# One block for messages, cross attention and the last self-attention: one queue per engine, eight pooled PSUM banks, key roots as logarithm and exponential

## What is computed

```python
x = x + L0_xattn(layernorm(x), ctx, ...)     # 4 layers: self attention, cross attention, gated FFN
x = x + L0_attn(layernorm(x), U, V)          # messages
x = x + L0_ffn(layernorm(x), W, disha)       # x @ W.T + pooled @ disha
x = x + L1_xattn(ctx, layernorm(x), mask)    # 64 latents on 1601 context rows and themselves
x = x + L1_attn(layernorm(x), Wqkv, Wo)      # causal self attention, 16 heads
x = x + L1_ffn(layernorm(x), gate, w1, w2)   # 8 experts, top 2

# messages, C = 16 blocks of R = 64
u, v = (z @ U.T) * s, (z @ V.T) * s
qh = sigmoid(u_c @ v_c.T)
G = ((qh @ v) @ U + (qh.T @ u) @ V) * s
# L1 cross attention, per batch
xn = layernorm(ctx) * gx + bx                # 1601 x 128
k = rmsnorm(xn @ Wk) ; q = rmsnorm(ln @ Wq)
attn = softmax(where(mask, q @ k.T, -inf))   # 2 heads of 64
```

## Time and profile before

| | us |
|---|---|
| median of three runs | 670.51 (663.33 to 674.94) |
| the profiled execution | 668.31 |
| its span, from first to last instruction | 666.4 |
| layers (with set-up) | 0 to 258 |
| messages and FFN | 261 to 347 |
| cross attention | 347 to 555 |
| last self-attention | 555 to 594.5 |
| experts | 594.5 to 666.4 |

### The profile page before, as it was taken

The page is one execution under the profiler, slowest core; times in us unless marked ns, Lnnn a source line. Parts: engine busy times, 40 slices in busy tenths (PEclk is TensorE's granted clock), DMA queues, the critical chain, the costliest instruction groups (busy, mean ns, idle before and its releaser), DMA issues. The chain is left out here.

```text
span 666.4 us, 13787 instructions
## 1 busy us (share of the span) xinstructions
PE 566.7 (85%) x5334; PEld 437.1 (66%) x5334; DVE 373.7 (56%) x957; ACT 233.6 (35%) x544; POOL 262.7 (39%) x350
## 2 busy tenths in 40 slices
PE   0889998999999893988757999899898966959997
PEld 0666865866696673777645777677686754536676
DVE  4576676665457764365643677655645653634342
ACT  1366356445443651332213433222222321421210
POOL 3562372255125511035543576937537412400000
PEclk9999999997599997899985999575767976978999
DMA  5501011010620002101110001011000000000000
GB/s 154 222 1 30 17 50 29 18 48 1 190 94 2 1 2 60 73 2 53 52 50 1 1 1 50 0 50 49 3 1 1 1 0 2 1 1 1 0 2 17
DMA packets 8488, 22.20 MB, mean 33 GB/s; under 512 B 1248, under 2 KB 4152, under 8 KB 8160
## 3 DMA queue, kind: packets, MB, share of 16 engines
q1 hardware_dynamic: 8416, 21.23, 9.7%
HBM read 20.97 MB, written 0.26 MB: 32 GB/s over the span
## 5 line engine op out<-in xcount | busy, mean ns | idle before, releaser
L823 POOL TENSOR_TENSOR rstd<-ss,par 128x1 f32<-128x1 f32 x52 | 28.5, 549 | 107.8 <-ACT sq L675 107.6
L1212 PE MATMUL sc<-rope,pr 128*128 128x128 f32 x208 | 58.3, 367 | 0.0
L1426 POOL TENSOR_TENSOR rk<-rk,par 128x8 f32<-128x8 f32 (+1 forms) x32 | 45.7, 1427 | 2.7
L1212 PEld LDWEIGHTS sc<-rope,pr 128*128 128x128 f32 x208 | 35.9, 217 | 8.2
L1349 DVE TENSOR_TENSOR sd<-sc,rk 128x512 f32<-128x512 f32 (+1 forms) x32 | 18.9, 591 | 37.8 <-PE sc L1212 16.4
L1284 ACT ACTIVATE pr<-pt 128x512 f32<-128x512 f32 (+1 forms) x32 | 16.5, 515 | 61.8 <-PE pt L1201 61.7
L1201 PE MATMUL pt<-xw,pr 128*128 128x128 f32 x208 | 36.9, 328 | 0.0
L1227 PE MATMUL pt<-xh,sd 128*128 128x130 f32 x208 | 34.3, 327 | 1.5 <-ACT sd L1288 1.5
L1201 PEld LDWEIGHTS pt<-xw,pr 128*128 128x128 f32 x208 | 33.1, 237 | 2.2 <-issue 1.1
L692 ACT ACTIVATE pr<-sd 128x1024 f32<-128x1024 f32 (+1 forms) x36 | 31.2, 866 | 9.5 <-DVE sd L770 7.2
L1227 PEld LDWEIGHTS pt<-xh,sd 128*128 128x128 f32 x208 | 32.5, 241 | 2.6 <-issue 2.5
(11 more groups left out here) (255 smaller groups left out, 1394.3 us busy)
## 6 DMA issues: line engine op xcount, KB each, us to landing
cx<-ctx_in SPq DMA_DIRECT2D x8, 768.0 KB
we<-we_in SPq DMA_DIRECT2D x8, 514.0 KB, 8.4
wc<-wc_in SPq DMA_DIRECT2D x4, 768.5 KB, 5.6
wa<-wa_in SPq DMA_DIRECT2D x5, 387.0 KB, 3.0
wb<-wb_in SPq DMA_DIRECT2D x4, 256.5 KB, 3.6
uvT<-uvT_in SPq DMA_DIRECT2D x1, 1024.0 KB, 4.7
uv<-uv_in SPq DMA_DIRECT2D x1, 1024.0 KB, 6.9
xw<-xw_in SPq DMA_DIRECT2D x1, 323.0 KB
```

The costliest lines, as they stand in the source:

```text
L823: nc.gpsimd.tensor_tensor(rstd[:, t:t + 1], ss[:, t:t + 1], par[:, 1:2], ALU.pow).then_inc(s[piece], 1)
L1212: last = nc.tensor.matmul(part, xnT[n % 3][:, P * j:P * j + P], qp[:, i, :, :].rearrange("p h q -> p (h q)"), start=False, stop=True, skip ...
L1426: nc.gpsimd.tensor_tensor(rk[:, n, 0:2 * w], rk[:, n, 0:2 * w], par[:, 1:2].to_broadcast([P, 2 * w]), ALU.pow).then_inc(xm[piece], 1)
```

## The change

- The middle block and the last self-attention become one block with one sorted queue per engine. The table YAT now holds the messages, the FFN, the cross attention and the last self-attention: pieces of a tile that come before cross attention (HEAD) with a step of 20.883 per tile, pieces of a batch (XWAY) with 16.435 per batch, pieces of a tile behind it (TAIL) with 32.87 per tile, and the moments and the scaling of context rows with steps of their own. Layernorms are done tile by tile (z_, f_, x_, l_, n_ moments, power, norm).
- All eight PSUM banks are one pool: each user takes one bank, or two next to each other for the messages, project and turn, and waits for the last users of just these.
- The first layernorm of tiles 0 to 2 (z_*) moves into the queues of the layers; that of tile 3 is in the new block.
- The root of the keys: POOL keeps the floor (c_floor), ACT takes the logarithm and then exp(-x/2) (c_root), with one table load behind the last tanh.
- `top` becomes c_top: six tensor_tensor maxima, the first as soon as two groups are there.
- notm and sel have 128 partitions instead of 8, the rows past 8 being zero.
- c_normed of batches 3 to 7 is no longer tied to c_moments of the same load: these batches are loaded twice, once for the moments and once for the scaling (LOADS; 13 loads instead of 8).
- Buffers move: xnT into wa[1] and new tiles, sT into the space of uvT and uv, others into rope, kblk, sd and pr. All loads of the block wait until POOL has cleared 79 semaphores (64 before, when only the context rows waited).

The diff, cut to its core:

```diff
-XSTEP = 10.99
-XAT = {
+YSTEP = {"HEAD": 20.883, "XWAY": 16.435, "TAIL": 32.870, "MOMENTS": 20.974, "NORMED": 14.636}
...
+    "PE": {"z_turn": -75.33, "across0": -58.75, "along0": -47.11, "along1": -54.15, "across1": -55.67, "M0": -38.77,
...
         self.bank = {}
+        free, last = [float("-inf")] * 8, [()] * 8
+        for _, i, g, p in self.queue["PE"]:
+            n = next((n for n in YBANKS if p in YBANKS[n]), 0)
+            if n and (p, g) not in [("sum_ctx", k) for k in range(1, 4)]:
+                k = min(range(0, 8, n), key=lambda k: max(free[k:k + n]))
...
-        mraw = xsb("mraw", [B, CT * P], U8)
-        notm = xsb("notm", [B, CT * P], BF16)
-        sel = xsb("sel", [B, B, P], BF16)
+        mraw = xsb("mraw", [P, CT * P], U8)
+        notm = xsb("notm", [P, CT * P], BF16)
+        sel = xsb("sel", [P, B, P], BF16)
...
         def x_sp(sp):
+            sp.wait_ge(s["x_raised"], 1)
...
-            for b in range(B):
-                if b >= 2:
-                    sp.wait_ge(s["c_center"], 4 * (b - 2) + 4)
+            for u, (_, b) in enumerate(LOADS):
+                if u >= 2:
+                    kind, k = LOADS[u - 2]
+                    sp.wait_ge(xm["c_moments" if kind == "stats" else "c_center"], 4 * k + 4)
...
+            elif piece == "c_root":
+                x_wait(act, "c_floor", n + 1)
+                part = rk[:, n, 0:2 * width(g)]
+                nc.scalar.activation(part, part, ACT.Ln).then_inc(xm["c_log"], 1)
+                x_wait(act, "c_log", n + 1)
+                nc.scalar.activation(part, part, ACT.Exp, scale=-0.5).then_inc(xm[piece], 1)
...
-            elif piece == "c_rnorm":
+            elif piece == "c_floor":
                 x_wait(pool, "c_sums", n + 1)
...
-                nc.gpsimd.tensor_tensor(rk[:, n, 0:2 * w], rk[:, n, 0:2 * w], par[:, 1:2].to_broadcast([P, 2 * w]), ALU.pow).then_inc(xm[piece], 1)
...
-                nc.vector.tensor_reduce(mxp[i % 2][:], sT[i % 2][:, 0:CT, :].rearrange("p c q -> p q c"), AX, ALU.max).then_inc(xm["top0"], 1)
+                    last = nc.vector.tensor_tensor(mxr[:], tiles[0], tiles[1], ALU.max)
```

More of the change, by code:

```diff
@@ L108, in __init__ @@
     def __init__(self, engines, when):
-        self.queue = {e: sorted((when(p, l, t), l, t, p) for p, layers in pieces for l in layers for t in range(T))
+        self.queue = {e: sorted((when(p, l, t), l, t, p) for p, layers in pieces for l in layers for t in range(T)
+                                if p[:2] != "z_" or t < T - 1)
                       for e, pieces in engines.items()}
@@ L181 @@
 class CrossOrder:
     def __init__(self):
[L185 to L186 removed]
+        self.queue = {e: sorted((x_late(p, i, g), i, g, p) for p in pieces for i in x_range(p) for g in range(len(YENDS[p])))
+                      for e, pieces in YAT.items()}
         self.bank = {}
[L188 to L194 removed]
@@ L197 @@
-XORDER = CrossOrder()
+        free, last = [float("-inf")] * 8, [()] * 8
[3 more added lines that the diff above has]
+                k = min(range(0, 8, n), key=lambda k: max(free[k:k + n]))
+                ends = [(f, i, x_final(f, g)) for f in YBANKS[n][p]]
+                self.bank[p, i, g] = k, n, sorted({e for b in range(k, k + n) for e in last[b]})
+                free[k:k + n] = [max(x_late(*e) for e in ends)] * n
+                last[k:k + n] = [tuple(ends)] * n
@@ L216, in program @@
         pt = ctx.enter_context(nc.psum_tensor("pt", [P, 1024], F32))
-        small = [ctx.enter_context(nc.psum_tensor(f"small{i}", [P, 512], F32)) for i in range(2)]
+        sm = ctx.enter_context(nc.psum_tensor("sm", [P, 1024], F32))
+        small = [sm[:, 512 * i:512 * i + 512] for i in range(2)]
         x = sb("x", [P, T, D])
@@ L1113, in c_tiles @@
             return slice(CG[g][0], CG[g][-1] + 1)
+        LOADS = [("both", b) for b in range(XAHEAD)] + [("stats", b) for b in range(XAHEAD, B)] + [("norm", b) for b in range(XAHEAD, B)]
         def x_sp(sp):
+            sp.wait_ge(s["x_raised"], 1)
             sp.dma_start(xw[:], xw_in).then_inc(xw_loaded, 16)
@@ L1467, in x_pool_start, with x_queue @@
+        def x_queue(eng, piece_of, layer_of, engine):
+            fresh = False
+            for _, i, g, p in LAST.queue[engine]:
+                if p not in EARLY and not fresh:
+                    eng.wait_ge(s["x_raised"], 1)
+                    eng.sem_inc(s["x_seen"], 1)
+                    fresh = True
+                if p in SELF:
+                    layer_of(eng, LAST, p, LAYERS, i)
+                else:
+                    piece_of(eng, p, i, g)
         def x_pool_start(pool):
-            for i in range(2):
-                nc.gpsimd.memset(cx[i][:, CT - 1, :], 0.0).then_inc(s["c_zeroed"], 1)
@@ L1470, in x_pool_start @@
             raise_xm(pool)
             pool.sem_inc(s["x_raised"], 1)
+            for i in range(2):
+                nc.gpsimd.memset(cx[i][:, CT - 1, :], 0.0).then_inc(xm["c_zeroed"], 1)
             for i in range(3):
@@ L1646, in am_pool @@
-        def am_pool(pool):
-            layernorm_pool(pool, 1)
-            x_pool_start(pool)
-            layernorm_pool(pool, 2)
+            for i in range(T):
+                last = nc.gpsimd.memset(rope[:, i, 2:4, :], NEG)
+            last.then_inc(xm["sl_set"], 1)
         with nc.Block() as block:
```

806 lines of the change are left out of this document (391 added, 415 removed), and 3 rows, old and new, of the table YBANKS.

## The result

The changed kernel takes 585.84 us, median of 4 runs (574.18 to 592.98), beside 668.82 us of the kernel before, median of 4 (663.33 to 674.94). Every ratio in this document is of the fast executions alone (here 0.864, 95% interval 0.851 to 0.878), not of the medians (0.876), which are of all executions and in a later set include two odd ones, 1614.23 us of the kernel before and 1574.75 us of the changed one. The profiled execution of the changed kernel took 592.78 us, its span is 590.7. The last G and the first mask matmul start 0.1 us apart; B is counted from the mask matmul, C from the last scores to the experts' layernorm.

A forecast was written before the change was run, and what follows sets the result against it. It took TensorE's idling and half clock (109 us), blamed on GpSimd's powers, as what could be won. First products at 277 + 68 + 136 + 40 + 71.9 = 593, with 1.9 around the span 595; forecast 596 us, range 565 to 636.

The forecast's parts named there:

- B: Stretch from the last tile's G to the last scores: 119 us of TensorE work, 136 us in time, range 122 to 152.
- C: Stretch from the last scores to the experts' layernorm: 40 us, range 36 to 48, against 58.5 before.
- The mask: Mask matmuls on 128 partitions: mask and score pair 0.33 us instead of 0.58, saving 25.5 us of TensorE.
- rival that the type is the cost: Mask matmuls keep their price because bf16 stands between fp32: 29 us more, 625 us; chance 0.11.
- The start: New block's start to first message products: context load issued at 266.5, first products at about 277 us, range 274 to 281.
- A: Stretch from first message products to the last tile's G: 59 us of TensorE at density 0.87, 68 us; range 62 to 74.
- denser than I think: Rival: TensorE 0.95 dense from first message products to last scores, 62 + 125 us; 579 to 565 in all; chance 0.06.
- Experts: The experts, from their layernorm to the end, stay as they are: 71.9 us.
- GpSimd: GpSimd's work from 258 us on falls from 159 to 113 us, as it loses 45.7 us of powers.
- What bounds the kernel before: Cross attention before: GpSimd, slowed by 45.7 us of powers, falls behind, TensorE stands, and the clock goes to 1.2 GHz.
- c_top: Maximum over context tiles as six pairwise maxima: about 2.7 us per batch against 3.3, saving 5 us on VectorE.
- The rival of the falling clock: TensorE idles at pooled banks or VectorE's queue, clock falls to 1.2 GHz: 40 us more, 636 us; chance 0.11.

The follow-up runs named there:

- both small edits undone: The changed kernel with the mask and its selector on 8 partitions and the key root as a power on GpSimd again: 602.3 us, ratio 0.910.

## Why the prediction was right, and where it was not

The whole, 596 (565 to 636), was near the measured 585.84, in part by luck, as the sum below shows. The sign, the worth of the mask and the full clock in B were right; what the prediction named as the cause of the idling before was not. By its steps:

- **The mask** (0.33 us per pair, 25.5 us of work, bounds 0 and 31): right. 0.33 measured, B 23.6 us longer without it. The rival that the type is the cost is out: the pair of bf16 and fp32 on 128 rows takes 0.33 us, the 0.107 of a transpose and the 0.225 of an fp32 product, and nothing between. The rule of the Trainium skill (TensorEngine Tiling (Array Packing), Key Properties) on draining at a change of mode agrees: 0.25 us is what the change of rows costs here per pair, there and back. That the cost is such a drain no run shows.
- **The start** (first products about 16 us behind the block's start): 19.1 measured. The step that failed is the price of the clears: 3.6 us assumed for 79, 5.1 measured (280.08 to 285.18); and mask and selector, which the change makes sixteen times larger, go ahead of the context in the DMA queues (2.1 us, by the run with 8 rows), so the load took 6.5 us from its issue (287.37 to 293.90) and not 4.5. "TensorE need not wait for the layernorm" holds for tiles 0 to 2; tile 3's power held VectorE 7.08 us ahead of the load, and once the load came early that wait set the start. The 277 us were missed by 22, of which 4 are this (25.3 us from the layers' last matmul instead of 21.2) and 18 the layers.
- **A** (68 us from the first products to the last G): 63.9. TensorE was busy 62.87 of 64.00 in it, not 0.87.
- **B** (119 us of work, 136 in time): 115.9 of work, 118.4 in time. This is the mis-sized term, by 18 us: I took the density between that of the layers and of the messages, 0.87, and it was 0.98. The case "denser than I think" was the nearer one for B (125) and A (62), and put too low at 0.06.
- **C** (40 us): 36.9. **Experts** 71.9: 72.3.
- With the measured 291.5 us behind the first products (63.9 + 118.4 + 36.9 + 72.3) the start I forecast gives 277 + 291.5 + 1.9 = 570. The layers of the profiled execution took 18 us more and the start 4, and the median of the four lies between: two errors of opposite sign, the layers' scatter and B, put 596 so near, and that is luck.
- **GpSimd** (113 us of work): 118.4. **ScalarE** (64 activations at 0.25): 0.20 to 0.21 each, 13.1 us in all. The table load, taken at 1 us, is in ScalarE's timeline of the changed kernel:

```profile
350.23 1.28 ACT L1390 ACT_TABLE_LOAD   x1
```

  The Trainium skill (ScalarE: Activation LUTs, What ACT_TABLE_LOAD costs) makes up its 2.7 us of about 1.28 us of load and 1.38 us of drain. The load agrees; the drain can't be seen here, since ScalarE then waits 2.77 us for TensorE (until 354.28), so that the switch held nothing up.
- **What bounds the kernel before** is where the argument was wrong. I read three waits of 8.0 us and 33.89 of 50 busy us as "GpSimd is the slow one", which "falls behind", so that "TensorE stands, and the clock goes to 1.2 GHz". Both steps fail. With GpSimd's powers gone from the old kernel nothing moved. And in the trace of before the order is the other way: the clock fell at 414.4, after 50.47 busy of 51.40 us, and the first wait came behind it. TensorE, then GpSimd, in the kernel before:

```profile
409.66 1.06 PE L1201 MATMUL pt<-xw,pr 128*128 128x128 f32 x8
...
415.16 2.07 PE L1201 MATMUL pt<-xw,pr 128*128 128x128 f32 x8
...
420.07 1.09 PE L1195 MATMUL small<-cf,xh 128*128 128x128 f32 x4 [2.63 <-POOL xh L1160]
```
```profile
415.04 0.20 POOL L1145 TENSOR_TENSOR rsx<-mvx,par 128x13 f32<-128x13 f32 x1 [4.12 <-DVE mvx L1139]
```

  The same eight instructions for the keys take twice as long before TensorE has waited as much as 1 us for anything. Of the four falls between 413 and 513 us three (414.4, 445.1, 503.2) came ahead of such a wait and one (475.8) inside it. GpSimd itself stood idle ahead of all three waits, 4.12, 8.72 and 11.84 us, for VectorE's moments of the context, which stood in VectorE's queue behind the 3.00 us maximum; no run tests that order by itself. The busy column had said what was the bound: 90.69 of 100 us of TensorE in the very stretch at 0.64, beside 61.02 of GpSimd. GpSimd became one only when the merged order and the mask had brought TensorE to 15 us per batch, which is why the root is worth 0.2 us alone and some 21 at the end. For the changed kernel "GpSimd's 11 us per batch against TensorE's 15" had the right order and too high a figure: 68.26 and 115.91 us over eight batches are 8.5 and 14.5.
- **c_top** (2.7 us, 5 us of VectorE saved): 3.65 us per batch measured, more than the 3.3 of the old form; its gain is the 3.6 us at the very end.
- **The rival of the falling clock** (636): did not come. B ran at 1.00. The Trainium skill (TensorE: Matmul & The Clock Gate, A second HAM failure mode: psum-queue depth-cycling) would have the pooled banks make the clock swing; this trace does not show it. The longest wait of TensorE in B was 0.5 us.
- **The merging** itself is the largest part: 402.4 to 334.3 us with both small edits undone, 68 of the 92 us; 18 of them lie ahead of the first mask matmul, 29 from there to the last scores, 22 in C, and the experts took 1 more. In the windows above TensorE's work at full clock, busy time by granted clock, is 128 us from first mask to last scores before, and 139 in the merged block with both edits undone, where the other tiles' self-attention runs beside the batches; and it took 173 and 144 us. The mean clock went from 0.79 to 0.98, and C, with one tile instead of four, went from 58.5 to 36.8. What in the merging does this stays open: one queue, pooled banks, layernorms tile by tile, the earlier moments and the second loads came together and none was taken out alone. That the density keeps the clock up was argued from both kernels' traces, not tested; the fall at 414.4 in dense work speaks against it as the whole reason.

## What to carry to other kernels

Count busy time and granted clock together before an engine is named the bound: one that is 91% busy at 0.64 is it, and a few short waits for another engine are not evidence against that. Look at what the awaited engine was itself waiting for, and whether the clock fell before the wait or after it. Where two engines need nearly the same time per step, an edit's worth must be tried with and without the other: here each alone brought 2 to 3 us and the pair 24. Here a wait at the head of a queue shrank when the chain behind it started sooner; moving the waiting work down the queue only moved the wait.

## What was not expected of the hardware

**Half clock in dense stretches.** The layers' own code differs in time by up to 25 us from execution to execution (in the ten traces with the merged block its first transpose comes between 255.5 and 280.1 us), and the granted clock tells where. The changed kernel's first trace, and the run with the mask on 8 rows, same windows in the layers:

```profile
50.00:80.00 30.00, 28.99 (x237) 21.99 (x237) 14.14 (x37) 13.88 (x42) 4.85 (x8) 0.68 0.08 20
...
110.00:140.00 30.00, 29.33 (x224) 20.62 (x222) 13.32 (x32) 13.43 (x38) 5.33 (x8) 0.60 0.06 16
```
```profile
50.00:80.00 30.00, 28.30 (x297) 23.45 (x297) 19.45 (x47) 16.53 (x53) 8.40 (x13) 1.00 0.09 26
...
110.00:140.00 30.00, 28.69 (x287) 23.79 (x286) 19.33 (x46) 14.38 (x46) 8.30 (x13) 1.00 0.09 26
```

TensorE is busy over 28 of 30 us in all four, and in two the clock is 0.60 to 0.68, so its busy share does not explain it. What does, stays open; no run here was made for it.

**VectorE stands for GpSimd's length.** A maximum of 128x128, both inputs in SBUF, takes 0.29 us alone and 1.01 to 1.15 beside a scaling of context rows. VectorE, then GpSimd, in the changed kernel's batch 4:

```profile
436.38 1.01 DVE L1555 TENSOR_TENSOR pr<-pr 128x128 f32<-128x128 f32 x1
437.43 1.15 DVE L1557 TENSOR_TENSOR pr<-pr,rope 128x128 f32<-128x128 f32 x1
438.71 0.29 DVE L1560 TENSOR_TENSOR pr<-pr,uvT 128x128 f32<-128x128 f32 x1
```
```profile
436.08 1.16 POOL L1207 TENSOR_TENSOR xh<-cx,mvx 128x512 f32<-128x512 f32 x1
437.39 1.04 POOL L1211 TENSOR_TENSOR xh<-xh,rsx 128x512 f32<-128x512 f32 x1
```

Each long one begins while a GpSimd operation runs and ends within 0.15 us of it; the third, with GpSimd idle, is short. This is the missing 1 us of c_top. The Trainium skill (SBUF — State Buffer, SBUF: two separate sides) says that GpSimd and a VectorE operation with two SBUF inputs take the same pair of ports, and that one holds it for its whole length; for the scaling of rows the trace agrees. For GpSimd's power it does not: that on 128x13, 2.45 us long at 433.66, did not lengthen the 128x512 maximum that ran at 434.38 (0.68 us), nor did the four others of B that ran beside a maximum.
